# A recurrent two-layer kernel: how the first groups and the weight maxima are prepared

## Chip, cores and metric

One core of one Trainium2 chip. The metric is the device time of one execution in microseconds (us), the median of several runs; lower is better.

## What is computed

```python
xn = layernorm(x)                                   # x: 32 x 256 x 128, f32
s = L0_attn(xn)       # mix with previous row, k, v, r products, exp, decayed sums over time, Wo
g = silu(L0_ffn(xn))  # three products with weights of +1/-1 (bools k0, k1, k2), relu between
x = x + s * g
xn = layernorm(x)
s = L1_attn(xn)       # W_in, conv, silu, W_x, softplus step, scan over time, W_out
g = silu(L1_ffn(xn))  # shared and 4 of 16 routed experts, gelu
x = x + s * g
```

Layer 1's weights are scaled by powers of two and split into two halves of 16 bits. The power comes from a bound on a tensor's magnitude (`amax`, seven tensors: I_IN, I_UP, I_RW, I_WX, I_DT, I_CW, I_CB).

## The kernel before

The 8192 rows of x are 16 groups of 512, all kept in SBUF. Each engine has its own list of instructions, written by hand, tied by semaphores. `bodies` runs `layer0(n)` for 18 values of n: three written out, a loop for n = 3 to 14, three more. In a body n every engine does its part for group f = n (normalised rows, products, scans), for m = n - 1 (hidden layers 2 and 3 of the ffn, division by the sums) and t = n - 2 (result turned back and added). `between` puts extra steps behind a body: on VectorE `magnitudes` behind body 0 and `scales` behind body 2, on GpSimd `constants` behind body 1. `paired` then runs layer 1.

Names: `xn` normalised rows; `b_T` the PSUM bank they are turned into; `prev` and `xh`, ScalarE's copies from it; `xm` the mix (VectorE, L726), the operand of the k, v, r products; `xl` the low half of the turned rows. `hidden0` and `hidden1` are the ffn's products. `high` (ScalarE) and `low` (VectorE, L717) split their results. `Pk`, `Pv` are the scans (L759, L766), `gp` and `sg` the body's end on VectorE (L777, L781). `w0` is made of `k0_u` and the signs of `scal`; `w1`, `w2` by GpSimd.

The loads stand on three queues: SP (x, `wsq` = Wk, Wv, Wr, Wo, then k0, then layer 1's), ScalarE (small vectors), GpSimd (k1, k2). `wq_loaded` covers the four square weights and k0; `wa_loaded` all six small loads.

## Time and profile before

| | |
|---|---|
| median of 3 runs | 714.25 us (711.76 to 715.2) |
| the profiled execution | 714.81 us |
| its span | 713.0 us |
| TensorE, VectorE, ScalarE, GpSimd busy | 643.3, 636.2, 504.4, 281.5 us |
| mean granted clock | 0.97 of full |

The span runs from the first to the last instruction. Busy time can overlap between engines. An idle time stands in brackets before the row that ended it, with the one that released it.

### The profile page before, as it was taken

The numbers are of one execution on the slowest core, as the hardware profiler recorded it, in microseconds if no ns is written. First come the engines' busy times: TensorE is split into PE (matmuls) and PEld (weight loads), VectorE is DVE, ScalarE is ACT, GpSimd is POOL, SyncE is SP. The second block draws the span as 40 slices with busy tenths as digits, with TensorE's granted clock in tenths as the row PEclk, the third lists the DMA queues.
The fourth block names the chain that finished last, engine by engine and source line by source line (L and its number), as shares of the span: only waits on it lengthen the run. The fifth ranks groups of instructions, "written<-read, shape, count | busy, mean of one in ns | idle before, by whom it ended". The sixth has DMA issues, their size and how long they took to land. (4 is left out here: it accounts for less than half of the span.)

```text
span 713.0 us, 10841 instructions
## 1 busy us (share of the span) xinstructions
PE 643.3 (90%) x2711; PEld 306.4 (43%) x2711; DVE 636.2 (89%) x1467; ACT 504.4 (71%) x800; POOL 281.5 (39%) x278
## 2 busy tenths in 40 slices
PE   2796899999999997679999999999999999999985
PEld 1342344444444443324444444444444444444432
DVE  5896999999999998658999999999999999999876
ACT  2463566666666664279788878888797888788874
POOL 6456576677777664013221231223032213312220
PEclk9898999999999999569999999999999999999999
DMA  5431000000000000000000000000000000000000
GB/s 143 115 86 44 0 0 0 0 0 0 0 0 0 0 1 0 1 0 1 0 16 15 1 15 15 15 1 15 15 15 0 15 15 0 15 15 15 0 16 29
DMA packets 10739, 11.29 MB, mean 16 GB/s; under 512 B 4800, under 2 KB 6288, under 8 KB 10720
## 3 DMA queue, kind: packets, MB, share of 16 engines
q1 hardware_dynamic: 9744, 10.73, 5.1%
q0 software_dynamic: 112, 0.33, 0.2%
q8 instruction: 8, 0.13, 0.1%
q10 hardware_dynamic: 864, 0.00, 0.1%
q14 instruction: 11, 0.09, 0.0%
HBM read 6.87 MB, written 4.19 MB: 16 GB/s over the span
## 5 line engine op out<-in xcount | busy, mean ns | idle before, releaser
L1058 PE MATMUL bank<-arena,w 128*128 128x512 f16 x640 | 153.9, 389 | 19.8 <-DVE arena L717 14.1
L1058 PE MATMUL bank<-arena,dnT 128*128 128x512 f32 x288 | 138.6, 592 | 0.0
L613 ACT ACTIVATE arena<-bank,xinv 128x512 f32<-128x512 f32 x144 | 94.9, 687 | 39.0 <-PE bank L1058 38.8
L443 POOL TENSOR_TENSOR arena<-arena 128x512 f32<-128x512 f32 x48 | 59.7, 1274 | 137.8 <-ACT arena L550 137.8
L1058 PEld LDWEIGHTS bank<-arena,w 128*128 128x128 f16 x640 | 63.4, 100 | 98.8 <-issue 24.3
L476 ACT ACTIVATE arena<-bank 128x512 f16<-128x512 f32 x96 | 53.9, 606 | 35.1 <-PE bank L1058 35.1
L433 POOL TENSOR_TENSOR arena<-arena 128x512 f32<-128x512 f32 x16 | 17.1, 1067 | 150.1 <-DVE arena L917 150.1
L1058 PE MATMUL bank<-arena,wsqT 128*128 128x512 f32 x128 | 65.9, 619 | 6.0 <-DVE arena L726 6.0
L1058 PEld LDWEIGHTS bank<-arena,dnT 128*128 128x128 f32 x288 | 53.7, 191 | 35.9 <-issue 21.4
L926 DVE SCALAR_TENSOR_TENSOR arena<-bank,cws,arena 128x506 f32<-128x506 f32 (+1 forms) x96 | 67.1, 740 | 1.1
L717 DVE SCALAR_TENSOR_TENSOR arena<-bank,arena 128x512 f16<-128x512 f32 x96 | 60.2, 670 | 1.7 <-ACT arena L476 0.5
L938 DVE TENSOR_TENSOR arena<-arena 128x512 f32<-128x512 f32 x80 | 52.4, 689 | 0.0
L396 POOL TENSOR_TENSOR arena<-arena 128x512 f16<-128x512 f32 x32 | 36.9, 1155 | 29.7 <-ACT arena L476 22.9
L473 ACT ACTIVATE arena<-bank 128x512 f32<-128x512 f32 x32 | 19.1, 597 | 33.0 <-PE bank L1058 33.0
L400 POOL TENSOR_TENSOR arena<-arena 128x512 f32<-128x512 f32 x16 | 20.3, 1270 | 51.1 <-DVE arena L753 51.1
L979 DVE TENSOR_TENSOR_SCAN arena<-arena 128x256 f32<-128x256 f32 x64 | 38.9, 671 | 0.0
L1058 PE MATMUL bank<-arena,wcH 128*128 128x512 f16 x128 | 38.1, 379 | 0.0
L1058 PE MATMUL bank<-xh,upH 128*128 128x512 f16 x72 | 28.8, 401 | 8.3 <-ACT arena L613 4.8
L1058 PEld LDWEIGHTS bank<-arena,wsqT 128*128 128x128 f32 x128 | 25.4, 200 | 22.9 <-issue 9.7
L588 ACT ACTIVATE arena<-arena 128x512 f32<-128x512 f32 x32 | 20.2, 631 | 20.3 <-DVE arena L926 20.3
L1058 PE MATMUL bank<-arena,w_out 128*128 128x512 f32 x64 | 30.2, 594 | 3.1 <-DVE arena L986 3.1
L1058 PE MATMUL bank<-xh_,upH 128*128 128x512 f16 x72 | 27.4, 380 | 5.0 <-ACT arena L613 5.0
(208 smaller groups left out, 1519.5 us busy)
## 6 DMA issues: line engine op xcount, KB each, us to landing
x_all<-in_L_attn_x SPq DMA_DIRECT2D x16, 256.0 KB, 2.7
out<-x_all SPq DMA_DIRECT2D x16, 256.0 KB, 2.0
up_n<-in_L_ffn_routed_up SPq DMA_DIRECT2D x1, 512.0 KB, 3.9
dn_n<-in_L_ffn_routed_down SPq DMA_DIRECT2D x1, 512.0 KB, 5.4
wx<-in_L_attn_W_x SPq DMA_DIRECT2D x1, 288.0 KB, 3.0
k_u<-in_L_ffn_k POOLq DMA_DIRECT2D x1, 256.0 KB, 5.1
w_in<-in_L_attn_W_in SPq DMA_DIRECT2D x1, 256.0 KB, 2.7
k_u<-in_L_ffn_k SPq DMA_DIRECT2D x1, 128.0 KB, 5.6
```

The lines of the kernel that those rows point to most:

```text
L396: g.tensor_tensor(hl[:, 1, j, :], relu[:, j, :], hh[:, 1, j, :], ALU.subtract).then_inc(sem["a_low"], 1)
L400: g.tensor_tensor(ya[:, :], ysr[:, :], rec[:, :], ALU.mult).then_inc(sem["a_y"], 1)
L443: g.tensor_tensor(prod[:, c, :], act[:, c + 1, :], gate[:, :], ALU.mult).then_inc(sem["b_actp"], 1)
L473: a.activation(relu[:, j, :], src, ACT.Relu).then_inc(sem["a_relu"], 1)
L476: a.activation(hh[:, layer, j, :], src, ACT.Relu).then_inc(sem[("a_hi0", "a_hi1")[layer]], 1)
L588: a.activation(xc[:, par, k, :], u[:, k, :], ACT.Silu).then_inc(sem["b_xc"], 1)
L613: a.activation(act[:, c, :], q_U[(c + 1) % 2][:, :], ACT.Gelu, scale=xinv[:, I_UP:I_UP + 1]).then_inc(sem["b_act"], 1)
L717: v.scalar_tensor_tensor(hl[:, layer, j, :], b_Z[layer][j][:, :], 0.0, hh[:, layer, j, :], ALU.max, ALU.subtract).then_inc(sem[("a_lo0", " ...
L926: v.scalar_tensor_tensor(uk, seqs(q_U[k][:, :])[:, :, 0:T - back], cws[:, k, t:t + 1], uk, ALU.mult, ALU.add)\
L938: v.tensor_tensor(prod[:, c, :], act[:, c + 1, :], gate[:, :], ALU.mult).then_inc(sem["b_actg"], 1)
L979: last = v.tensor_tensor_scan(H[:, k, w], delta[:, k, w], bx[:, k, w], 0.0, ALU.mult, ALU.add)
L1058: return nc.tensor.matmul(ps, lhsT, rhs, start=start, stop=stop)
```

## The change

- Loads: `k0` is issued between Wv and Wr, with a semaphore of its own; Wr and Wo have one too. On ScalarE's queue the mix comes first, then the three scalars, then decay and first; each part has its semaphore.
- Group 0: GpSimd computes only rstd; VectorE normalises with four instructions.
- The square weights are turned in two halves, and ScalarE copies them out (VectorE did all four).
- In body 0, `w0` comes behind `xm` and `xl`; `high` and `low` of hidden layer 1 and the decays come ahead of the scans. ScalarE makes its channel factors behind `xh`.
- `up_n`, `rw_n` and `wdt` get as bound the sum of magnitudes in a partition (ScalarE, in body 1) instead of the maximum.
- GpSimd's `partition_all_reduce` goes. TensorE turns `amax` in body 1, VectorE takes the largest in each of seven rows and puts it on a diagonal, TensorE spreads it by a product with ones, VectorE copies it out. `scales` stands behind body 1 instead of body 2.

VectorE at the opening, before (`c` is c3, `w` is w0, the last row is xm):

```order
L700 TENSOR_SCALAR w0c<-sg_ 128x1
L701 TENSOR_TENSOR w0d<-k_u 128x512
L702 TENSOR_TENSOR sab<-scal,sg_ 128x2
L703 TENSOR_SCALAR w<-w0d,w0c 128x512
L704 TENSOR_TENSOR c<-sab 128x1
L706 COPY wsqT<-bank 128x512
L709 SCALAR_TENSOR_TENSOR c<-c,scal 128x1
L710 TENSOR_SCALAR dec<-ones,tch 128x128
L711 TENSOR_SCALAR dec<-ones,tch 128x128
L712 TENSOR_SCALAR c<-c 128x1
L726 SCALAR_TENSOR_TENSOR arena<-bank,chan,prev 128x512
```

and now:

```order
L734 TENSOR_SCALAR xn<-x_all,mv,rstd 128x128 x4
L740 TENSOR_SCALAR w1c<-sg_ 128x1
L741 TENSOR_SCALAR w1c<-sg_ 128x1
L742 TENSOR_TENSOR sab<-scal,sg_ 128x2
L743 TENSOR_SCALAR w0c<-sg_ 128x1
L746 TENSOR_TENSOR w0d<-k_u 128x512
L778 SCALAR_TENSOR_TENSOR arena<-bank,chan,prev 128x512
L781 SCALAR_TENSOR_TENSOR xl<-bank,xh 128x512
L752 TENSOR_SCALAR w<-w0d,w0c 128x512
L753 TENSOR_TENSOR c<-sab 128x1
```

Ahead of xm the copy of wsqT, w0, c3 and the decays are gone, and the normalising rows have come.

GpSimd from body 1 to body 2, before:

```order
L409 TENSOR_TENSOR arena<-arena,Pv 128x512
L412 TENSOR_TENSOR arena<-arena 128x512
L424 ISA
L424 ISA amax<-amax 128x7
L396 ISA
L396 TENSOR_TENSOR arena<-arena 128x512 x2
L400 TENSOR_TENSOR arena<-arena 128x512
```

and now:

```order
L422 TENSOR_TENSOR arena<-arena,Pv 128x512
L425 TENSOR_TENSOR arena<-arena 128x512
L409 TENSOR_TENSOR arena<-arena 128x512 x2
L413 TENSOR_TENSOR arena<-arena 128x512
L366 TENSOR_TENSOR ve<-mv,epsc 128x4
```

The reduction and the two other `ISA` rows around it are gone; the rest keeps its order.

The diff, cut to its core:

```diff
         loads_q = [(wsq[:, i, :], A["L0_attn_" + n]) for i, n in enumerate(("Wk", "Wv", "Wr", "Wo"))]
-        loads_q.append((k0_u[:, :, :], A["L0_ffn_k0"].rearrange("(k p) f -> p k f", p=P)))
+        loads_r = loads_q[2:]
+        loads_q = loads_q[:2]
+        load_k0 = (k0_u[:, :, :], A["L0_ffn_k0"].rearrange("(k p) f -> p k f", p=P))
+        load_mix = (chan[:, 2:3], A["L0_attn_time_mix"].rearrange("a b c -> c (a b)"))
         loads_a = [
-            (chan[:, 2:3], A["L0_attn_time_mix"].rearrange("a b c -> c (a b)")),
             (chan[:, 0:1], A["L0_attn_time_decay"]),
             (chan[:, 1:2], A["L0_attn_time_first"]),
         ]
-        loads_a += [(scal[:, i:i + 1], A["L0_ffn_" + n].partition_broadcast(P)) for i, n in enumerate(("s0", "s1", "s2"))]
+        loads_s = [(scal[:, i:i + 1], A["L0_ffn_" + n].partition_broadcast(P)) for i, n in enumerate(("s0", "s1", "s2"))]
...
+            sp.dma_start(*load_k0).then_inc(sem["k0_loaded"], 16)
+            for dst, src in loads_r:
+                sp.dma_start(dst, src).then_inc(sem["wr_loaded"], 16)
...
-                    pool.wait_ge(sem[ph + "centred"], n + 1)
+                    pool.wait_ge(sem[ph + "centred"], n)
...
-            normalise(0, "a_")
+            spread_of_rows(0, "a_")
...
-            def constants():
-
-                pool.wait_ge(sem["absmax_ready"], NSC)
-                g.partition_all_reduce(amax[:, :], amax[:, :], P, bass.bass_isa.ReduceOp.max).then_inc(sem["absmax_all"], 1)
-
-            bodies(pool, layer0, {1: constants, G - 1: lambda: spread_of_rows(0)})
+            bodies(pool, layer0, {G - 1: lambda: spread_of_rows(0, "b_")})
...
+            actv.dma_start(*load_mix).then_inc(sem["mix_loaded"], 16)
+            for dst, src in loads_s:
+                actv.dma_start(dst, src).then_inc(sem["scal_loaded"], 16)
             for dst, src in loads_a:
                 actv.dma_start(dst, src).then_inc(sem["wa_loaded"], 16)
-            actv.wait_ge(sem["wa_loaded"], WA_ALL)
-
+
+            def square_out(half):
+
+                actv.wait_ge(sem["square_turned"], half + 1)
+                a.activation(wsqT[:, 2 * half:2 * half + 2, :].rearrange("p a b -> p (a b)"),
+                             (b_S, b_F)[half][:, 0:2 * P], ACT.Copy).then_inc(sem["square_ready"], 1)
+
+            square_out(0)
+            actv.wait_ge(sem["scal_loaded"], WS_ALL)
             a.activation(sg_[:, :], scal[:, 0:2], ACT.Sign).then_inc(sem["signs_ready"], 1)
-            a.activation(tch[:, 0:1], chan[:, 0:1], ACT.Exp).then_inc(sem["chan_ready"], 1)
-            actv.wait_ge(sem["chan_ready"], 1)
-            a.activation(tch[:, 1:2], tch[:, 0:1], ACT.Exp, scale=-1.0).then_inc(sem["chan_ready"], 1)
-            a.activation(tch[:, 2:3], chan[:, 1:2], ACT.Exp).then_inc(sem["chan_ready"], 1)
             actv.wait_ge(sem["mix_ready"], 1)
 
+            def channel_factors():
+
+                actv.wait_ge(sem["wa_loaded"], WA_ALL)
+                a.activation(tch[:, 0:1], chan[:, 0:1], ACT.Exp).then_inc(sem["chan_ready"], 1)
+                actv.wait_ge(sem["chan_ready"], 1)
+                a.activation(tch[:, 1:2], tch[:, 0:1], ACT.Exp, scale=-1.0).then_inc(sem["chan_ready"], 1)
+                a.activation(tch[:, 2:3], chan[:, 1:2], ACT.Exp).then_inc(sem["chan_ready"], 1)
+                square_out(1)
...
+            def bounds():
+
+                flat = "p a b -> p (a b)"
+                actv.wait_ge(sem["wb_loaded"], WB_ALL)
+                actv.wait_ge(sem["const_ready"], 9)
+                for i, w, at in ((I_UP, up_n[:, :, :].rearrange(flat), 0), (I_RW, rw_n[:, :], UC * P),
+                                 (I_DT, wdt[:, :], (UC + 1) * P)):
+                    a.activation(absw[0:w.shape[0], at:at + w.shape[1]], w, ACT.Abs,
+                                 accum_out=amax[0:w.shape[0], i:i + 1]).then_inc(sem["absmax_ready"], 1)
...
+                    if isinstance(f, int) and f == 0:
+                        channel_factors()
...
+                if isinstance(f, int) and f == 1:
+                    bounds()
                 if has(m):
                     high(1, m, 2)
+                if isinstance(f, int) and f == 0:
+                    for j in range(FC):
+                        high(0, 0, j)
...
-            dve.wait_ge(sem["wa_loaded"], WA_ALL)
+            dve.wait_ge(sem["mix_loaded"], 16)
             v.tensor_scalar(tch[:, 3:4], chan[:, 2:3], -1.0, 1.0, ALU.mult, ALU.add).then_inc(sem["mix_ready"], 1)
 
+            def normalised(n, ph):
+
+                dve.wait_ge(sem[ph + "rstd"], n + 1)
+                after(dve, sem[ph + "xnT"], n)
+                for j in range(J):
+                    last = v.tensor_scalar(xn[:, j, :], x_all[:, bass.ds(n * N + j * P, P)], mv[:, j, 0:1],
+                                           rstd[:, j:j + 1], ALU.subtract, ALU.mult)
+                last.then_inc(sem[ph + "xn"], 1)
+
+            normalised(0, "a_")
             dve.wait_ge(sem["signs_ready"], 1)
             v.tensor_scalar(w1c[:, 0:1], sg_[:, 1:2], 2.0 * W1S, None, ALU.mult)
             v.tensor_scalar(w1c[:, 1:2], sg_[:, 1:2], -W1S, None, ALU.mult).then_inc(sem["w1_ready"], 1)
-            dve.wait_ge(sem["wq_loaded"], WQ_ALL)
-
-            links(v.tensor_scalar(w0c[:, :], sg_[:, 0:1], 2.0 * W0S, None, ALU.mult),
-                  v.tensor_tensor(w0d[:, :], k0_u[:, 0, :], k0_u[:, 1, :], ALU.subtract),
-                  v.tensor_tensor(sab[:, :], scal[:, 0:2], sg_[:, :], ALU.mult))
-            links(v.tensor_scalar(w0[:, :], w0d[:, :], w0c[:, 0:1], None, ALU.mult),
-                  v.tensor_tensor(c3[:, 0:1], sab[:, 0:1], sab[:, 1:2], ALU.mult))
-            dve.wait_ge(sem["square_turned"], 1)
-            v.tensor_copy(wsqT[:, :, :].rearrange("p a b -> p (a b)"), b_S[:, :]).then_inc(sem["square_ready"], 1)
-            dve.wait_ge(sem["const_ready"], 7)
-            dve.wait_ge(sem["chan_ready"], 3)
-            links(v.scalar_tensor_tensor(c3[:, 1:2], c3[:, 0:1], FS, scal[:, 2:3], ALU.mult, ALU.mult),
-                  v.tensor_scalar(dec[:, 0:P], ones[:, :], tch[:, 1:2], None, ALU.mult),
-                  v.tensor_scalar(dec[:, P:T], ones[:, 0:T - P], tch[:, 1:2], None, ALU.mult))
-            v.tensor_scalar(c3[:, 2:3], c3[:, 1:2], 0.5, None, ALU.mult).then_inc(sem["const_done"], 1)
+            v.tensor_tensor(sab[:, :], scal[:, 0:2], sg_[:, :], ALU.mult)
+            v.tensor_scalar(w0c[:, :], sg_[:, 0:1], 2.0 * W0S, None, ALU.mult).then_inc(sem["signs_used"], 1)
+            dve.wait_ge(sem["const_ready"], 5)
+            dve.wait_ge(sem["k0_loaded"], 16)
+            v.tensor_tensor(w0d[:, :], k0_u[:, 0, :], k0_u[:, 1, :], ALU.subtract).then_inc(sem["k0_joined"], 1)
+
+            def signed_weights():
+
+                dve.wait_ge(sem["signs_used"], 1)
+                dve.wait_ge(sem["k0_joined"], 1)
+                links(v.tensor_scalar(w0[:, :], w0d[:, :], w0c[:, 0:1], None, ALU.mult),
+                      v.tensor_tensor(c3[:, 0:1], sab[:, 0:1], sab[:, 1:2], ALU.mult))
+                v.scalar_tensor_tensor(c3[:, 1:2], c3[:, 0:1], FS, scal[:, 2:3], ALU.mult,
+                                       ALU.mult).then_inc(sem["const_done"], 1)
+
+            def decays():
+
+                dve.wait_ge(sem["const_ready"], 7)
+                dve.wait_ge(sem["chan_ready"], 3)
+                dve.wait_ge(sem["const_done"], 1)
+                v.tensor_scalar(c3[:, 2:3], c3[:, 1:2], 0.5, None, ALU.mult)
+                v.tensor_scalar(dec[:, 0:P], ones[:, :], tch[:, 1:2], None, ALU.mult)
+                v.tensor_scalar(dec[:, P:T], ones[:, 0:T - P], tch[:, 1:2], None, ALU.mult).then_inc(sem["const_done"], 1)
...
+                    if isinstance(f, int) and f == 0:
+                        v.scalar_tensor_tensor(xl[:, :], b_T[:, :], XS, xh[:, :], ALU.mult,
+                                               ALU.subtract).then_inc(sem["a_xl"], 1)
+                        signed_weights()
...
+                if isinstance(f, int) and f == 0:
+                    for j in range(FC):
+                        low(0, 0, j)
+                    decays()
+                    dve.wait_ge(sem["const_done"], 2)
...
+                if isinstance(f, int) and f == 1:
+                    largest()
...
-                for i, w in ((I_IN, w_in[:, :]), (I_UP, up_n[:, :, :].rearrange(flat)), (I_RW, rw_n[:, :]),
-                             (I_WX, wx[:, :, :].rearrange(flat)), (I_DT, wdt[:, :]),
+                for i, w in ((I_IN, w_in[:, :]), (I_WX, wx[:, :, :].rearrange(flat)),
                              (I_CW, cw[:, :, :].rearrange(flat)), (I_CB, cb[:, :])):
                     v.tensor_reduce(amax[0:w.shape[0], i:i + 1], w, AX.X, ALU.max,
                                     apply_absolute_value=True).then_inc(sem["absmax_ready"], 1)
 
+            def largest():
+
+                dve.wait_ge(sem["absmax_turned"], 1)
+                link(v.tensor_reduce(amx[0:NSC, :], b_S[0:NSC, 0:P], AX.X, ALU.max))
+                v.tensor_scalar(adiag[0:NSC, :], ident[0:NSC, 0:NSC], amx[0:NSC, 0:1], None,
+                                ALU.mult).then_inc(sem["absmax_diag"], 1)
...
+                dve.wait_ge(sem["absmax_spread"], 1)
+                v.tensor_copy(amax[:, :], b_RX[:, 0:NSC]).then_inc(sem["absmax_all"], 1)
                 dve.wait_ge(sem["absmax_all"], 1)
...
-            bodies(dve, layer0, {0: magnitudes, 2: scales, G - 1: matrices, G: turned_matrices})
+            bodies(dve, layer0, {0: magnitudes, 1: scales, G - 1: matrices, G: turned_matrices})
...
-            for i in range(4):
-                last = nc.tensor.transpose(b_S[:, i * P:(i + 1) * P], wsq[:, i, :], ident[:, :])
-            last.then_inc(sem["square_turned"], 1)
+
+            def square_turned(half):
+
+                for i in range(2):
+                    last = nc.tensor.transpose((b_S, b_F)[half][:, i * P:(i + 1) * P], wsq[:, 2 * half + i, :], ident[:, :])
+                last.then_inc(sem["square_turned"], 1)
+
+            square_turned(0)
...
+                if isinstance(f, int) and f == 0:
+                    pe.wait_ge(sem["wr_loaded"], WR_ALL)
+                    square_turned(1)
...
+                    if isinstance(t, int) and t == 0:
+                        pe.wait_ge(sem["absmax_all"], 1)
...
+                if isinstance(f, int) and f == 1:
+                    pe.wait_ge(sem["absmax_ready"], NSC)
+                    pe.wait_ge(sem["square_ready"], 1)
+                    nc.tensor.transpose(b_S[0:NSC, 0:P], amax[:, :], ident[:, :]).then_inc(sem["absmax_turned"], 1)
...
+                    if isinstance(f, int) and f == 0:
+                        pe.wait_ge(sem["square_ready"], 2)
...
                     last.then_inc(sem["a_f"], 1)
                 if has(m):
                     pe.wait_ge(sem["a_y"], m + 1)
+                    if isinstance(m, int) and m == 0:
+                        pe.wait_ge(sem["absmax_diag"], 1)
                     after(pe, sem["a_sg"], m)
                     mm(b_S[:, :], wsqT[:, 3, :], ya[:, :]).then_inc(sem["a_s"], 1)
+                if isinstance(f, int) and f == 1:
+                    pe.wait_ge(sem["a_thr"], 2)
+                    mm(b_RX[:, 0:NSC], ones[0:NSC, :], adiag[0:NSC, :]).then_inc(sem["absmax_spread"], 1)
```

## Rows read from the trace of the kernel before

**Rows 1.** The page: busy time of the engines, and TensorE's granted clock in 40 slices.
```profile
PE 643.3 (90%) x2711; PEld 306.4 (43%) x2711; DVE 636.2 (89%) x1467; ACT 504.4 (71%) x800; POOL 281.5 (39%) x278
...
PEclk9898999999999999569999999999999999999999
```

**Rows 2.** Timeline of the loop: start us, us, engine, line, operation, [idle before].
```profile
103.41 0.75 DVE L726 SCALAR_TENSOR_TENSOR arena<-bank,chan,prev 128x512 f32<-128x512 f32 x1 [0.22 <-ACT xh L486]
...
117.03 0.66 PE L1069 MATMUL bank<-ident,xn 128*128 128x128 f32 x4 [0.60 <-POOL xn L368]
...
118.93 0.75 DVE L726 SCALAR_TENSOR_TENSOR arena<-bank,chan,prev 128x512 f32<-128x512 f32 x1 [0.21 <-ACT xh L486]
```

**Rows 3.** Timeline of VectorE, opening.
```profile
8.86 0.15 DVE L693 TENSOR_SCALAR tch<-chan 128x1 f32<-128x1 f32 x1 [3.74 <-DMA scal<-in_L_ffn_s]
...
10.08 2.09 DVE L703 TENSOR_SCALAR w<-w0d,w0c 128x512 f16<-128x512 f32 x1
...
13.93 0.74 DVE L726 SCALAR_TENSOR_TENSOR arena<-bank,chan,prev 128x512 f32<-128x512 f32 x1
```

**Rows 4.** Timeline of VectorE, end of body 0.
```profile
23.16 2.45 DVE L717 SCALAR_TENSOR_TENSOR arena<-bank,arena 128x512 f16<-128x512 f32 x4
...
26.13 1.34 DVE L791 TENSOR_REDUCE amax<-up_n 128x1 f32<-128x1152 f32 x1
...
28.70 0.73 DVE L726 SCALAR_TENSOR_TENSOR arena<-bank,chan,prev 128x512 f32<-128x512 f32 x1
```

**Rows 5.** Timeline of all engines, body 2.
```profile
45.15 0.75 DVE L726 SCALAR_TENSOR_TENSOR arena<-bank,chan,prev 128x512 f32<-128x512 f32 x1 [0.21 <-ACT xh L486]
...
61.23 3.77 PE L1058 MATMUL bank<-arena,w 128*128 128x512 f16 x8 [5.65 <-POOL arena L396]
...
65.76 0.69 DVE L777 SCALAR_TENSOR_TENSOR gp<-thf,bank 128x512 f32<-128x512 f32 x1 [6.69 <-ACT thf L520]
...
67.15 0.94 DVE L807 SCALAR_TENSOR_TENSOR bnd<-amax 128x1 f32<-128x1 f32 x1
...
72.72 0.75 DVE L726 SCALAR_TENSOR_TENSOR arena<-bank,chan,prev 128x512 f32<-128x512 f32 x1
...
73.53 1.98 PE L1058 MATMUL bank<-arena,wsqT 128*128 128x512 f32 x4 [1.96 <-DVE arena L726]
```

**Rows 6.** Timeline of GpSimd, TensorE and ScalarE, opening.
```profile
6.59 1.03 POOL L363 TENSOR_TENSOR xn<-x_all,mv 128x512 f32<-128x512 f32 x1
7.77 1.04 POOL L368 TENSOR_TENSOR xn<-xn,rstd 128x512 f32<-128x512 f32 x1
...
9.63 1.06 PE L1069 MATMUL bank<-ident,xn 128*128 128x128 f32 x4
...
11.38 0.59 ACT L486 ACTIVATE xh<-bank 128x512 f16<-128x512 f32 x1
...
14.73 4.49 PE L1058 MATMUL bank<-arena,wsqT 128*128 128x512 f32 x6 [4.04 <-DVE arena L726]
```

**Rows 7.** Timeline of GpSimd around its reduction over partitions.
```profile
52.69 0.40 POOL L424 PARTITION_ALL_REDUCE amax<-amax  x1 [5.86 <-issue]
59.95 1.14 POOL L396 TENSOR_TENSOR arena<-arena 128x512 f16<-128x512 f32 x1 [6.86 <-issue]
```

**Rows 8.** Timeline of VectorE: four normalising instructions, beside GpSimd's and alone.
```profile
277.49 2.79 DVE L891 TENSOR_SCALAR xn<-x_all,mv,rstd 128x128 f32<-128x128 f32 x4 [1.41 <-POOL rstd L419]
...
330.42 1.11 DVE L891 TENSOR_SCALAR xn<-x_all,mv,rstd 128x128 f32<-128x128 f32 x4
```

**Rows 9.** Instructions of L759: duration ns min/median/max, first and last start us.
```profile
L759 DVE TENSOR_TENSOR_SCAN Pk<-dec,arena x32: 660/682/1461, 19.1 to 268.4; 128x256 f32<-128x256 f32 x32
```

**Rows 10.** Body 1: timeline of TensorE and ScalarE; windows, with the granted clock before DMA share.
```profile
25.76 6.55 PE L1058 MATMUL bank<-arena,w 128*128 128x512 f16 x16 [4.38 <-DVE arena L717]
...
35.79 0.60 ACT L476 ACTIVATE arena<-bank 128x512 f16<-128x512 f32 x1 [1.70 <-PE bank L1058]
...
25.00:26.00 1.00, 0.24 (x1) 0.14 (x2) 1.00 (x3) 0.00 (x0) 0.90 (x1) 0.50 0.00 0
```

More of the change, by code:

```diff
@@ L507, in layer0 @@
                     a.activation(thr[:, :], b_RX[:, :], ACT.Tanh, scale=0.5).then_inc(sem["a_thr"], 1)
-                    high(0, f, 0)
+                    if not (isinstance(f, int) and f == 0):
+                        high(0, f, 0)
                     actv.wait_ge(sem["a_thr"], f + 1)
@@ L511, in layer0 @@
                     a.activation(sr[:, :], thr[:, :], ACT.Copy, scale=0.5, bias=0.5).then_inc(sem["a_sr"], 1)
-                    high(0, f, 1)
-                    high(0, f, 2)
-                    high(0, f, 3)
+                    if not (isinstance(f, int) and f == 0):
+                        high(0, f, 1)
+                        high(0, f, 2)
+                        high(0, f, 3)
                 if has(m):
@@ L732, in layer0 @@
                         dve.wait_ge(sem["bn_done"], f + 2)
-                    after(dve, sem["a_z0"], FC * f)
-                    v.scalar_tensor_tensor(xl[:, :], b_T[:, :], XS, xh[:, :], ALU.mult, ALU.subtract).then_inc(sem["a_xl"], 1)
+                    if not (isinstance(f, int) and f == 0):
+                        dve.wait_ge(sem["a_z0"], FC * f)
+                        v.scalar_tensor_tensor(xl[:, :], b_T[:, :], XS, xh[:, :], ALU.mult,
+                                               ALU.subtract).then_inc(sem["a_xl"], 1)
                     if ahead:
@@ L768, in layer0 @@
                     last.then_inc(sem["a_scanV"], 1)
+                if has(f) and not (isinstance(f, int) and f == 0):
                     low(0, f, 0)
                     low(0, f, 1)
-                if has(f):
                     low(0, f, 2)
@@ L884, in turned_low @@
                 v.scalar_tensor_tensor((xl, xl_)[par][:, :], ps[:, :], XS, (xh, xh_)[par][:, :], ALU.mult, ALU.subtract).then_inc(sem["b_xl"], 1)
-            def normalised(n):
-                dve.wait_ge(sem["b_rstd"], n + 1)
-                after(dve, sem["b_xnT"], n)
-                for j in range(J):
-                    last = v.tensor_scalar(xn[:, j, :], x_all[:, bass.ds(n * N + j * P, P)], mv[:, j, 0:1],
-                                           rstd[:, j:j + 1], ALU.subtract, ALU.mult)
-                last.then_inc(sem["b_xn"], 1)
-            bodies(dve, layer0, {0: magnitudes, 2: scales, G - 1: matrices, G: turned_matrices})
+            bodies(dve, layer0, {0: magnitudes, 1: scales, G - 1: matrices, G: turned_matrices})
             def top_four(n):
@@ L1018, in layer1 @@
                 if ahead:
[L1019 removed]
+                    normalised(f + 1, "b_")
                 if has(m):
```

32 lines of the change are left out of this document (16 added, 16 removed).

## The prediction

> **What bounds the kernel now.** I read the busy shares and slices first [rows 1]. TensorE and VectorE are each busy for nine tenths of the span. The granted clock of TensorE is at or near full in all 40 slices but those at the change of layers, with lower digits in the first slices too. So I asked where the first 75 us differ from the loop of layer 0. In the loop, the addition that makes xm (L726) comes every 15.52 us [rows 2]. I use this instruction on VectorE as the mark of a body: it starts body 0 at 13.93, body 1 at 28.70, body 2 at 45.15 and body 3 at 72.72 [rows 3 to 5]. The bodies before the loop thus take 14.77, 16.45 and 27.57 us. Two losses stand out. The first mark comes only at 13.93, though xn was ready at 7.77 + 1.04 = 8.81 and xh at 11.38 + 0.59 = 11.97 [rows 6]: VectorE was busy with weights. And body 2 is 12 us longer than a loop body. There GpSimd's reduction over partitions stands with 5.86 us of idle time before it and 6.86 after it, both put down to "issue" and not to another engine [rows 7]. Behind it TensorE waits 5.65, and VectorE 6.69 [rows 5]. After these, VectorE's chain of scales runs from 67.15 to the mark at 72.72, some 5.5 us [rows 5].
>
> Nothing after body 3 is changed but the order of source lines. A body there is held by the engines, not by loads, so I take what is gained up to body 3 to be gained at the end. The change is therefore summed at the marks.
>
> **1. The first mark.** Rstd is there at 6.59, where GpSimd's own subtraction starts [rows 6]. GpSimd then took 2.2 us for two steps. VectorE's four instructions take 1.11 us when left alone and 2.79 at worst, at a place where GpSimd worked beside them [rows 8]. GpSimd now clears buffers at that time, so I take 1.6, with 1.1 and 2.8 as ends: xn at 8.2. TensorE no longer turns four square matrices just before (two are turned earlier, since it waits for Wk and Wv only); turning xn takes 1.06 and ended at 10.69 [rows 6], so 9.4. ScalarE's two passes end 11.97 - 10.69 = 1.3 later, at 10.7. VectorE has by then only small instructions and w0d behind it, and w0, with its 2.09 us [rows 3], stands after xm and xl. Mark 0 comes at 10.9 instead of 13.93: **-3.0** (-1.8 to -3.6). This needs the signs, whose three loads are now issued second to fourth in ScalarE's queue; before they landed by 8.86 at the latest [rows 3], and even that would be no later than 8.9.
>
> **2. Body 0.** Xm ends at 11.6, and three f32 products take 4.3 to the first hidden one, as before (14.73 to 19.05, by the 4.49 of its six records) [rows 6]: 16.0. The first hidden product and ScalarE's half bring low() to 17.1; four of them take 2.45 [rows 4] and now stand ahead of the scans: 19.5. The decay tables, 0.6, make 20.1. Four scans take 0.66 to 1.46 each [rows 9], 2.6 to 4.2 in all; I take 3.3: 23.4. The seven maxima took 28.70 - (23.16 + 2.45) = 3.1. Three of them, with 1152 + 128 + 256 = 1536 elements a partition, go to ScalarE; the largest took 1.34 [rows 4], so the three some 1.8, and about 1.4 is left. Mark 1: 24.9, a body of 14.0 instead of 14.77: **-0.8** (-1.7 to +0.2). Hidden products of body 1 wait for low(), 19.5 instead of 25.61, so that TensorE is idle for about 1 us where it was for 4.4 [rows 10].
>
> **3. Body 1 without scales.** Sixteen hidden products took 6.55 us there at the clock of 0.50 [rows 10]; with the shorter gap they should keep full clock. Then the body is a loop body, 15.5. Added on VectorE are largest() (two tiny instructions of some 0.15 [rows 3] and two waits, 0.5), on TensorE a turn of seven columns and a 7-column product (under 0.5 together). ScalarE's three sums of magnitudes have 1536 elements. By the 0.60 us of 512 elements they cost 1.8; they stand where ScalarE sat idle for 1.70 [rows 10], so 0 to 0.5 of it shows. Body 1: 16.0 instead of 16.45: **-0.45** (-0.9 to +0.5).
>
> **4. Scales come before mark 2.** The copy from PSUM adds 0.3. The chain took 5.5, partly since small instructions were held while GpSimd worked: one of a single element took 0.94 [rows 5], another such 0.15 [rows 3]. With its four long ones at 0.15, it would be some 2.1. After sg of body 1 GpSimd still has two or three instructions to run, so I take 4.3: **+4.6** (+2.4 to +5.8).
>
> **5. Body 2.** 27.57 less the chain of 5.5 and the idle 6.7 leaves 15.3, which agrees with a loop body: **-12.3** (-12.0 to -12.5). GpSimd's reduction is gone from the program, not moved, as the order of GpSimd's instructions shows. This is the term that carries the rest, so its cause matters. The row shows one idle stretch ahead of the reduction and one behind it, 12.7 us with nothing to wait for, and the next instruction, at 59.95, is what TensorE waited for. The Trainium skill, "GPSIMD Engine Reference", section "Instruction dispatch", prices the first call of a freshly loaded kernel at about 6 us, with no instruction in the profile. It names one such load, so by it alone GpSimd would be free at about 53, no engine would have waited, and the saving would be near 6 us less; the trace shows the second stretch as well and decides.
>
> Sum: -3.0 - 0.8 - 0.45 + 4.6 - 12.3 = **-11.95**. The profiled execution took 714.81 us (span 713.0), so 702.9. That run stands 0.56 above the median of 714.25, so the forecast for the median is **702.3 us**. Loads have slack: those of stage two are issued when s1W is cleared, now some 2 us earlier, since GpSimd no longer normalises first, and the maxima ask for them about 2 us earlier. They are hidden in both; if one landed later, body 0 would stretch by its lateness.
>
> **Rivals.**
> *A: the clock falls in the gap of the scales.* After sg TensorE has at most sixteen hidden products and a turn left. Sixteen at full clock take half of 6.55, 3.3; part of the first eight is done by then, so 2.9, while VectorE needs 0.3 + 4.3 + 0.75 to the next xm: idle 2.5 us. At mark 3 TensorE waited 1.96, and its next products ran at 1.98 for four records [rows 5]; a wait of 4.4 was followed by 0.50 [rows 10]. The gap lies between. If the clock falls, a stretch like the 6.55 of sixteen products is half lost, 3.3 at most; with some slack I take 2.5: 702.3 + 2.5 = 704.8. The Trainium skill, "TensorE: Matmul & The Clock Gate", section "HAM oscillation — how this bites in real kernels", says that waits of a kernel can bring the clock down again after each burst; the two rows above agree.
> *B: the start gains little.* If the signs land late or xn is held by the clears, terms 1 and 2 shrink to 1: 705.
> *C: the reduction's stall was not all code loading.* If something of GpSimd's after it is still late, say half of it, the gain is 5 to 6: 708.5.
> *D, slower: the loop runs in a worse phase.* In the loop TensorE waits 0.60 for xn and VectorE 0.21 for xh in each body [rows 2]. The engines hand over in a circle (xn, turned rows, xm, low), and a different entry could settle at another period, say with xn late by one GpSimd instruction (1.04 us [rows 6]). Over 12 loop bodies a period above 16.5 would take all of the 12 us; at 16.6 the time is 715.3. Against it: body 1, whose clock was down, and body 2, whose GpSimd stood still, both led into a loop of one period, so the circle sets it and not its entry.
> *E: no effect,* the saved time is waited for elsewhere, in the change of layers. Its code there waits for no load that lands so late.
>
> **How the numbers follow.** The forecast with its own range, 699.5 to 704: 0.55. A 0.20, B 0.10, C 0.08, D 0.03, E 0.04. The bounds of the terms, if all fall the same way, sum to -16.3 and -7.3, which is 698.0 and 707.0 for the median. I take these as the range: it holds the forecast, A and B, and leaves out C, D and E (0.15). Half a per cent, 3.6 us, is about what a measurement can tell from no change. Faster by more (below 710.7): 0.93; within: 0.04; slower: 0.03.
>
> **What would show it.** The marks should stand near 10.9, 24.9, 45.5 and 60.8. GpSimd's row should have no idle of "issue" over 5 us. VectorE's gap of 6.69 before gp should be gone, hidden products of body 1 should take 3.6 and not 6.55 for 16, and loop marks should stay 15.52 apart. I am wrong if mark 3 is later than 65, or if the loop's period moves by over 0.1 us.

## The result, and the profile after

The changed kernel takes **701.83 us** (median of 4 runs, 700.39 to 703.48) where the kernel before takes 714.25. The ratio of the two, taken over their runs, is 0.9839, with a 95% interval of 0.9803 to 0.9875 (the two medians alone divide to 0.983). The forecast was 702.3 with a range of 698 to 707. The profiled execution took 703.48 us; its span is 701.7, where that of before was 713.0. One run of `reduction_back` (812.34 us, mean granted clock 0.829) was in a slower state of the chip and is left out of its numbers below.

The page, busy time and granted clock, for comparison with [rows 1]:

```profile
PE 641.6 (91%) x2714; PEld 305.8 (44%) x2714; DVE 631.5 (90%) x1470; ACT 507.1 (72%) x808; POOL 279.7 (40%) x275
...
PEclk9999999999999997679999999999999999999999
```

No engine does much less than before: VectorE 4.7 us less, TensorE 1.7. Most of the 11.3 us is idle time that went: 9.6 us of TensorE's, 6.6 of VectorE's. The marks (start of the xm instruction on VectorE, now L778) say where. Timeline of VectorE, the marks of bodies 0 to 4, against [rows 3 to 5]:

```profile
10.75 0.75 DVE L778 SCALAR_TENSOR_TENSOR arena<-bank,chan,prev 128x512 f32<-128x512 f32 x1 [0.68 <-ACT xh L511]
...
25.83 0.73 DVE L778 SCALAR_TENSOR_TENSOR arena<-bank,chan,prev 128x512 f32<-128x512 f32 x1
...
45.92 0.74 DVE L778 SCALAR_TENSOR_TENSOR arena<-bank,chan,prev 128x512 f32<-128x512 f32 x1
...
61.01 0.75 DVE L778 SCALAR_TENSOR_TENSOR arena<-bank,chan,prev 128x512 f32<-128x512 f32 x1 [0.22 <-ACT xh L511]
...
76.53 0.75 DVE L778 SCALAR_TENSOR_TENSOR arena<-bank,chan,prev 128x512 f32<-128x512 f32 x1 [0.22 <-ACT xh L511]
```

| stretch | before | forecast | after |
|---|---|---|---|
| start to mark 0 | 13.93 | 10.9 | 10.75 |
| body 0 | 14.77 | 14.0 | 15.08 |
| body 1 (the scales stand here now) | 16.45 | 20.6 | 20.09 |
| body 2 (they stood here before) | 27.57 | 15.3 | 15.09 |
| body 3 | 15.16 | as before | 15.52 |
| sum, mark 4 | 87.88 | | 76.53 (-11.35) |

The loop's bodies stay 15.52 us apart, and the whole run is 714.81 - 703.48 = 11.33 shorter: between these two profiles nothing is gained or lost behind mark 4 (626.93 us from there to the end before, 626.95 after). So the time came from body 2 (-12.5) and the opening (-3.2), and body 1, which now holds the scales, took 3.6 of it back.

GpSimd's timeline shows the two idle stretches of [rows 7] gone. Its last instruction of body 1 and the first behind it:

```profile
41.31 1.27 POOL L425 TENSOR_TENSOR arena<-arena 128x512 f32<-128x512 f32 x1
44.83 1.15 POOL L409 TENSOR_TENSOR arena<-arena 128x512 f16<-128x512 f32 x1 [2.24 <-ACT arena L491]
```

It waits 2.24 us, and for ScalarE's data instead of for "issue". The chain of scales on VectorE, its first and its last instruction, the one long one:

```profile
42.98 0.16 DVE L880 SCALAR_TENSOR_TENSOR bnd<-amax 128x1 f32<-128x1 f32 x1
...
44.88 1.12 DVE L897 SCALAR_TENSOR_TENSOR fac<-fac,inv 128x1 f32<-128x1 f32 x1
```

From 42.98 to the mark at 45.92 it takes 2.94, where it took 5.57 before (67.15 to 72.72). Only one of its 16 instructions is held, and that one lies exactly beside GpSimd's at 44.83: they end at 46.00 and 45.98. The other 15 take 0.12 to 0.23 each.

One thing in the profile was not forecast. Timeline of TensorE in bodies 0 and 1, and windows of 1 us (the granted clock stands before the DMA share):

```profile
11.55 5.49 PE L1122 MATMUL bank<-arena,wsqT 128*128 128x512 f32 x6 [1.15 <-DVE arena L778]
...
20.82 3.61 PE L1122 MATMUL bank<-arena,w 128*128 128x512 f16 x16 [1.56 <-DVE arena L769]
26.62 3.18 PE L1122 MATMUL bank<-arena,wsqT 128*128 128x512 f32 x4 [2.18 <-DVE arena L778]
29.60 4.15 PE L1122 MATMUL bank<-arena,w 128*128 128x512 f16 x16
```

```profile
27.00:28.00 1.00, 1.00 (x3) 0.33 (x2) 0.48 (x3) 0.00 (x0) 1.00 (x2) 0.63 0.57 215
28.00:29.00 1.00, 1.00 (x3) 0.37 (x2) 1.00 (x6) 0.87 (x2) 1.00 (x2) 0.50 0.03 8
29.00:30.00 1.00, 1.00 (x2) 0.15 (x1) 1.00 (x1) 1.00 (x4) 0.44 (x1) 0.50 0.44 154
```

The sixteen hidden products of body 1 run at full clock, as hoped (3.61 instead of 6.55). But VectorE still has scans and maxima to do, TensorE waits 2.18 for xm, and the clock then falls to its lower level, 1.2 GHz (0.50 in the windows), under the k product. And the three f32 products of body 0 took 5.49 where the same six records had 4.49 before [rows 6].

### The profile page after: what moved, and what is told of

The parts are those of the page before. It is cut to its first block and busy times, and to the rows that moved or that the text cites. A ratio compares the mean times of both kernels' runs of the same rounds, so it can differ in the third digit from the quotient of the medians.

```text
span 701.7 us, 10854 instructions
## 1 busy us (share of the span) xinstructions
PE 641.6 (91%) x2714; PEld 305.8 (44%) x2714; DVE 631.5 (90%) x1470; ACT 507.1 (72%) x808; POOL 279.7 (40%) x275
## 5 line engine op out<-in xcount | busy, mean ns | idle before, releaser
L1122 PE MATMUL bank<-arena,w 128*128 128x512 f16 x640 | 149.7, 382 | 12.9 <-DVE arena L769 12.9
L1122 PE MATMUL bank<-arena,wsqT 128*128 128x512 f32 x128 | 67.6, 634 | 4.4 <-DVE arena L778 4.4
L368 POOL TENSOR_TENSOR rstd<-ve,neghalf 128x4 f32<-128x4 f32 x32 | 36.4, 1136 | 2.5
```

Source lines behind the costliest of these rows:

```text
L368: g.tensor_tensor(rstd[:, :], ve[:, :], neghalf[:, :], ALU.pow).then_inc(sem[ph + "rstd"], 1)
L1122: return nc.tensor.matmul(ps, lhsT, rhs, start=start, stop=stop)
```

## The experiments

The kernel before, measured beside them, had medians of 714.37 (13 runs) for the first four, 713.31 (11 runs) for the next four, and 710.2 (one run) for the last four. So times of different groups are compared by their ratios to it, and only with care by themselves.

### The reduction put back

`reduction_back` is the changed kernel with the reduction of before:

```diff
-            bodies(pool, layer0, {G - 1: lambda: spread_of_rows(0, "b_")})
+            bodies(pool, layer0, {1: constants, G - 1: lambda: spread_of_rows(0, "b_")})
...
-            bodies(dve, layer0, {0: magnitudes, 1: scales, G - 1: matrices, G: turned_matrices})
+            bodies(dve, layer0, {0: magnitudes, 2: scales, G - 1: matrices, G: turned_matrices})
```

`constants` is that of before; TensorE's turn and spreading, largest() and the copy are left out.

> The changed kernel with GpSimd's reduction over partitions back behind body 1 and the scales behind body 2; all else stays changed, the sums of magnitudes on ScalarE too. Theory (the stall is made by the reduction alone, its 5.86 and 6.86 us of issue around it): GpSimd shows both stretches again, mark 3 comes some 12 to 13 us after that of the changed kernel less the moved chain, so near 69 to 70, and the time is 710 to 711. Rival (the new opening had already made room, so the reduction would now be hidden): under 705. Rival (the opening carries the gain): 702.

Measured: 707.87 us (three runs, 706.95 to 708.12), ratio 0.9905 (0.987 to 0.9939), and marks at 10.59, 25.48, 42.37 and 68.83. Mark 3 is 7.8 us behind that of the changed kernel. Timeline of GpSimd, and mark 3 on VectorE:

```profile
48.32 0.40 POOL L430 PARTITION_ALL_REDUCE amax<-amax  x1 [6.16 <-issue]
56.04 2.26 POOL L409 TENSOR_TENSOR arena<-arena 128x512 f16<-128x512 f32 x2 [7.32 <-issue]
```

```profile
68.83 0.75 DVE L783 SCALAR_TENSOR_TENSOR arena<-bank,chan,prev 128x512 f32<-128x512 f32 x1
```

Both stretches are back. Mark 3 came within 0.2 us of its forecast; the time came lower than forecast by more than 2 us. The trace says where: layer 1's code is the same, but the stretch from its first product to the first of its second group took 18.37 us in this execution and 21.27 in the profile of the changed kernel. A mark's gain or loss does not reach the end whole in every execution (more on this in the last section).

### The reduction exchanged alone

`reduction_only` is the kernel before, with nothing but the reduction taken over from the change (turn, largest(), spreading, copy) and the scales behind body 1. Opening, loads and maxima are those of before.

> The kernel before with only the reduction exchanged for the turn, the largest, the diagonal and the spread, and the scales behind body 1; opening, maxima and body 0 as before. Theory: marks 0 and 1 stay at 13.93 and 28.70, mark 3 comes at about 64, the time is 714.3 less 8 to 9, so 705 to 706. Rival (reduction and opening only pay together): 710 or more.

Measured: 704.8 us (702.48 to 707.07), ratio 0.9857 (0.9822 to 0.9893). Marks 0 and 1 stayed, at 13.79 and 28.45. Timeline of VectorE, marks 2 and 3:

```profile
49.31 0.74 DVE L723 SCALAR_TENSOR_TENSOR arena<-bank,chan,prev 128x512 f32<-128x512 f32 x1
...
64.41 0.75 DVE L723 SCALAR_TENSOR_TENSOR arena<-bank,chan,prev 128x512 f32<-128x512 f32 x1 [0.22 <-ACT xh L483]
```

Mark 3 is 72.72 - 64.41 = 8.3 us earlier. With the 3.9 that `reduction_back` has at its mark 3 (72.72 - 68.83), the two halves give 12.2; the whole change gave 72.72 - 61.01 = 11.7. So the parts hardly touch each other, and the exchange of the reduction, with the move of the scales that it allows, is worth two thirds and more of the change at the marks.

### The reduction done twice

`reduction_twice` is the kernel before with the reduction's line written twice, one behind the other; VectorE's scales wait for both:

```diff
                 g.partition_all_reduce(amax[:, :], amax[:, :], P, bass.bass_isa.ReduceOp.max).then_inc(sem["absmax_all"], 1)
+                pool.wait_ge(sem["absmax_all"], 1)
+                g.partition_all_reduce(amax[:, :], amax[:, :], P, bass.bass_isa.ReduceOp.max).then_inc(sem["absmax_all"], 1)
```

> The kernel before with the reduction written twice in a row (the second leaves the maxima as they are). If the 5.86 and 6.86 us are paid at the change between GpSimd's own code and the reduction's, once in and once out, the second costs about its 0.4 us: 714.5 to 715.5. If each reduction pays them, a second costs 12 us more: 726 to 727. If the stretch behind is the reduction's own unseen work, it comes again and the stretch ahead does not: some 721.

Measured: 714.06 us (10 runs), ratio 1.0009 (0.9991 to 1.0028). Timeline of GpSimd:

```profile
51.28 0.40 POOL L424 PARTITION_ALL_REDUCE amax<-amax  x1 [5.77 <-issue]
51.78 0.38 POOL L426 PARTITION_ALL_REDUCE amax<-amax  x1
59.45 2.26 POOL L396 TENSOR_TENSOR arena<-arena 128x512 f16<-128x512 f32 x2 [7.29 <-issue]
```

The second reduction takes 0.38 us and has no stretch of its own. So the price is not that of a reduction. It is paid on the way into this kind of instruction (5.8 to 6.2 us in these profiles) and once more on the way back to ordinary ones (6.9 to 7.3). The unnamed `ISA` rows in the order of GpSimd's instructions before stand at these two places, one ahead of the reduction and one ahead of L396. What GpSimd does in the stretches no profile shows, and no run shows whether a later reduction, with ordinary instructions between, pays the first stretch again. Here a reduction of seven columns held GpSimd for 13 us.

### All maxima on VectorE

`maxima_vector` is the changed kernel with the three sums taken from ScalarE; VectorE takes all seven maxima again behind body 0.

> The changed kernel with all seven maxima on VectorE, true maxima as before. Theory: mark 1 comes 1.8 us later (27.6 instead of 25.83), TensorE waits longer before the k product of body 1, and the time rises by 1 to 2 us to 703 to 704. Rival (mark 1 is set by TensorE's slow products, VectorE had room): no change, 701.8.

Measured: 705.59 us (700.08 to 708.59), ratio 0.9875 (0.9813 to 0.9938), too wide to part it from the changed kernel by time. The trace is clearer. From the first maximum to mark 1 VectorE needs 26.59 - 23.45 = 3.14, in the changed kernel 25.83 - 24.46 = 1.37: 1.77 us less. Mark 1 came only 0.76 later, though, and not the 1.8 of the theory, since the first three products took 4.59 in this execution and not 5.49. This was the first sign that a part of body 0 differs from one execution to the next. TensorE's wait before the k product grew from 2.18 to 3.95, as the theory had it, and mark 3 came at 62.71, 1.70 later.

### The scales one body later

`scales_late` leaves the copy from PSUM behind body 1, and puts the chain of scales behind body 2.

> The changed kernel with the chain of scales behind body 2 again, where it stood before; the copy of the spread maxima stays behind body 1. Theory of the forecast (the chain's length is a matter of what GpSimd runs beside it): in the changed kernel it took 2.94 us (42.98 to 45.92), at the old place it takes 3 to 5.5, mark 3 comes 0 to 2.5 us later, and the time is 702 to 704. Rival (the place does not matter, each body has the same slack): same chain, same time within 0.5.

Measured: 704.66 us (703.1 to 707.53), ratio 0.9875 (0.9837 to 0.9914). Timeline of VectorE, the chain's long instructions and mark 3:

```profile
57.24 0.64 DVE L883 SCALAR_TENSOR_TENSOR bnd<-amax 128x1 f32<-128x1 f32 x1
...
58.02 1.22 DVE L885 TENSOR_TENSOR bnd<-bnd,amax 128x1 f32<-128x1 f32 x1
...
59.68 0.97 DVE L889 TENSOR_SCALAR inv<-pow 128x7 f32<-128x7 f32 x1
...
61.70 0.75 DVE L778 SCALAR_TENSOR_TENSOR arena<-bank,chan,prev 128x512 f32<-128x512 f32 x1
```

GpSimd beside it:

```profile
56.69 1.18 POOL L422 TENSOR_TENSOR arena<-arena,Pv 128x512 f32<-128x512 f32 x1
57.95 1.27 POOL L425 TENSOR_TENSOR arena<-arena 128x512 f32<-128x512 f32 x1
59.48 1.15 POOL L409 TENSOR_TENSOR arena<-arena 128x512 f16<-128x512 f32 x1 [0.26 <-ACT arena L491]
```

The same chain takes 61.70 - 57.24 = 4.46 us here and 2.94 in the changed kernel, with the same instructions. In its place behind body 2, GpSimd works at 56.69 to 60.6 with one gap of 0.26; behind body 1 it sits idle from 42.58 to 44.83. And the three long instructions end at 57.88, 59.24 and 60.65, where GpSimd's end at 57.87, 59.22 and 60.63. The four long ones of the kernel before end in the same way, 0.01 to 0.02 us behind one of GpSimd's each (68.09 behind 68.08, 72.00 behind 71.98). So an instruction of VectorE is held until GpSimd's is through, and what the chain costs is set by what GpSimd does beside it. Which of the small instructions are held and which pass beside a running one of GpSimd, these rows do not explain.

### Keeping TensorE's clock up

Three kernels add unused products, whose results nothing reads. `warm_opening` has ten products of the identity by itself before TensorE's first turn; `warm_both` has also eight f16 products ahead of the k product of body 1; `warm_all` has also 32 where TensorE is idle at the change of layers, and 14 ahead of the first expert:

```diff
+            for _ in range(10):
+                mm(b_Z0[:, 0:P], ident[:, :], ident[:, :])
...
+                if isinstance(f, int) and f == 1:
+                    for _ in range(8):
+                        mm(b_F[:, :], w1[:, 0, 0:P], hh[:, 0, 0, :])
...
+                if isinstance(f, int) and f == G:
+                    for _ in range(32):
+                        mm(b_T[:, :], w1[:, 0, 0:P], hh[:, 0, 0, :])
...
+                if isinstance(f, int) and f == 0:
+                    for _ in range(14):
+                        mm(q_F[:, :], upH[:, 0:P], XH[:, :])
```

> The changed kernel with ten products of ident with itself (f32, 128 columns, into a bank that is free) on TensorE between ident and the first turned weights; their result is not used. Theory (body 0 was 1 us longer than forecast since the three f32 products ran at half rate, 0.86 us from record to record, after an opening with no products): the products take 2.6 to 4.5 us instead of 5.3, mark 1 comes 0.8 to 2.5 us earlier, mark 3 as much. Rival (the engine slows again before 11.55, or low() and the scans wait for ScalarE): marks unchanged.

> As warm_opening, and eight unused f16 products ahead of the k product of body 1, where the changed kernel shows a granted clock of 0.50 from 28 to 30. Theory: that clock stays 1.00, the k and v products take 1.9 instead of 3.2 us, low() of body 1 does not wait 0.73 us for ScalarE, and mark 2 comes 0.5 to 1 us earlier than in warm_opening. Rival (VectorE sets body 1 alone): mark 2 as in warm_opening.

> As warm_both, and 32 unused products in the gap of the change of layers (TensorE idle 7.86 us before 278.48 in the changed kernel), 14 before the first expert of layer 1. Theory (runs of one kernel differ by 3 us with the mean granted clock, 0.977 against 0.984, and the marks of layer 0 do not move, so the change of layers is where they differ): the clock stays up through it, the time falls by 2 to 4 us against warm_both, to 695 to 698, and its runs spread by less than 2 us. Rival (VectorE bounds the change of layers): under 1 us.

| kernel | median us | runs | ratio to before (95%) |
|---|---|---|---|
| `warm_opening` | 701.4 | 699.91 to 703.07 | 0.9841 (0.9811 to 0.987) |
| `warm_both` | 698.94 | 697.74 to 700.25 | 0.98 (0.9772 to 0.9828) |
| `warm_all` | 698.29 | 698.03 to 698.75 | 0.9795 (0.9768 to 0.9821) |

In the first profile of `warm_opening` the clock stayed full in body 1 and mark 3 came at 58.76, 2.25 us before that of the changed kernel. Yet its ratio, 0.9841, was no better than the changed kernel's 0.9839. `warm_both` had mark 2 at 43.59 and `warm_opening` at 43.66: no gain there, but both profiles had full clock in body 1, so the pair does not test its theory. `warm_all` fills the gap at the change of layers. Timeline of TensorE there, the changed kernel first and `warm_all` second:

```profile
278.48 1.89 PE L1122 MATMUL bank<-arena,w 128*128 128x512 f16 x4 [7.86 <-DVE arena L769]
280.16 1.92 PE L1122 MATMUL bank<-arena,wsqT 128*128 128x512 f32 x2
```

```profile
275.55 1.20 PE L1122 MATMUL bank<-arena,w 128*128 128x512 f16 x4 [0.96 <-DVE arena L769]
276.59 1.02 PE L1122 MATMUL bank<-arena,wsqT 128*128 128x512 f32 x2
```

The idle 7.86 is filled, and the two products behind it take 1.02 instead of 1.92. The clock does not stay up through the whole change of layers, though: it reads 0.50 from 282 to 288. The six runs of `warm_all` lie within 0.7 us, where those of every other kernel but `reduction_back` (1.2) spread over 2.5 us and more. Its median is the lowest, but only 0.65 under that of `warm_both`, as the rival had it, and the intervals of these two overlap almost wholly. Measured at the same time, each of its six runs lies under the lowest of `warm_opening` (699.91), so unused products do pay once they stand in the later gaps too. That it beats the changed kernel itself is likely and not shown: they were not measured together, and the intervals 0.9768 to 0.9821 and 0.9803 to 0.9875 overlap a little.

### The same kernels profiled again

`warm_opening` had an earlier mark 3 and yet no better median, so both kernels were profiled again. `after_again` and `after_third` are the changed kernel, `warm_again` and `warm_third` are `warm_opening`, all with nothing edited.

> The changed kernel unchanged, profiled again. Four kernels with the same opening show the three f32 products of body 0 with 5.49, 5.35, 4.77 and 4.59 us for the same six records. Theory V (the step to full rate comes at a time that varies from one execution to the next): the row again lies between 4.5 and 5.5, another value than 5.49, and mark 1 moves by the difference, 24.9 to 25.8. Theory F (it belongs to the code): 5.4 to 5.5 and mark 1 at 25.8 again. Body 1: a granted clock of 0.50 for 2 us or more between 26 and 31, by both.

> As after_again, a third profile of the changed kernel. Theory V: the products' row between 4.5 and 5.5; theory F: 5.4 to 5.5. The clock's fall in body 1 is there again if it belongs to the code.

> The kernel of warm_opening (ten unused products ahead of the first turns), profiled again. If the unused products are what keeps body 1 at full clock: no 1 us window under 1.00 between 24 and 32, first three products 4.5 to 4.6, mark 3 at 58.5 to 59.0, 2 us before the changed kernel's. If it was luck: a fall in one of the two profiles, and products of up to 5.5.

> As warm_again, a third profile of it: full clock in body 1 and mark 3 at 58.5 to 59.0 by the one theory, a fall and mark 3 at 60 to 61 by the other.

| profile | us | three f32 products of body 0 | clock of 0.50 between marks 1 and 2 | marks 1, 2, 3 | body 1 |
|---|---|---|---|---|---|
| after | 703.48 | 5.49 | 27 to 31 | 25.83, 45.92, 61.01 | 20.09 |
| `after_again` | 700.71 | 4.69 | 39 to 43 | 24.86, 43.33, 58.43 | 18.47 |
| `after_third` | 701.91 | 5.30 | 26 to 31 | 25.52, 45.61, 60.70 | 20.09 |
| `warm_opening` | 699.98 | 4.54 | none | 24.27, 43.66, 58.76 | 19.39 |
| `warm_again` | 703.71 | 4.54 | 25 to 29 | 24.39, 44.48, 59.58 | 20.09 |
| `warm_third` | 699.61 | 2.84 | 24 to 28 | 23.22, 43.31, 58.41 | 20.09 |
| `warm_both` | 700.25 | 4.49 | none | 24.20, 43.59, 58.69 | 19.39 |
| `warm_all` | 698.11 | 4.54 | 39 to 43 | 24.51, 42.97, 58.08 | 18.46 |

The rows of body 0 in the changed kernel, 5.49, 4.69 and 5.30, bear out theory V: the same code takes different times.

Timeline of TensorE, the f32 products of bodies 0 and 1, in `after_again`:

```profile
11.44 4.69 PE L1122 MATMUL bank<-arena,wsqT 128*128 128x512 f32 x6 [1.03 <-DVE arena L778]
...
25.65 1.98 PE L1122 MATMUL bank<-arena,wsqT 128*128 128x512 f32 x4 [2.18 <-DVE arena L778]
```

in `warm_again`:

```profile
11.12 4.54 PE L1122 MATMUL bank<-arena,wsqT 128*128 128x512 f32 x6 [1.42 <-DVE arena L778]
...
25.18 3.68 PE L1122 MATMUL bank<-arena,wsqT 128*128 128x512 f32 x4 [2.19 <-DVE arena L778]
```

and in `warm_third`:

```profile
10.94 2.84 PE L1122 MATMUL bank<-arena,wsqT 128*128 128x512 f32 x6 [1.90 <-DVE arena L778]
...
24.01 3.45 PE L1122 MATMUL bank<-arena,wsqT 128*128 128x512 f32 x4 [2.18 <-DVE arena L778]
```

The reader should compare the brackets: TensorE waits 2.18 or 2.19 for the k product of body 1 in every one of them, and what follows runs at full clock in one execution (1.98) and mostly at half in the next (3.45, 3.68). The same code and the same wait give either. The early fall is thus no property of the changed kernel; it came in two of its three profiles, and in two of the three of `warm_opening`. That products in the opening keep body 1 at full clock, as the first profile of `warm_opening` suggested, is refuted with it. What they do change in each of its three profiles is the first turns (two square turns 0.38 instead of 0.69) and mark 0, 10.14 to 10.31 instead of 10.64 to 10.75; a gain of that size is under what the medians can show. The products of `warm_both` stand in the gap itself, which leaves 0.46 of it, and in both profiles with them (`warm_both`, `warm_all`) the k product runs at full clock; two profiles are too few to say that it always does.

The third profile of the changed kernel without an early fall, `after_again`, is not at full clock throughout. There the clock falls later in body 1, behind waits of 1.07 and 0.89 us; the same fall stands in `warm_all`, while the same two waits led to none in `warm_opening`. TensorE and GpSimd in `after_again`, and window 40 to 41:

```profile
39.49 3.37 PE L1122 MATMUL bank<-arena,w 128*128 128x512 f16 x8 [0.89 <-DVE arena L769]
...
44.23 1.16 POOL L409 TENSOR_TENSOR arena<-arena 128x512 f16<-128x512 f32 x1 [2.72 <-ACT arena L491]
```

```profile
40.00:41.00 1.00, 1.00 (x4) 0.35 (x3) 0.93 (x4) 0.00 (x0) 0.92 (x2) 0.50 0.68 156
```

Eight hidden products take 3.37 there and 1.90 in the profile of after. Yet body 1 is shortest in these two executions, 18.5 us, and not in the two at full clock, 19.39. The cause is the chain of scales. In `warm_opening`, at full clock, GpSimd gets its data in time to start in the middle of the chain, and VectorE is held; VectorE and GpSimd there:

```profile
42.29 1.05 DVE L893 TENSOR_TENSOR fac<-inv,bnd 128x1 f32<-128x1 f32 x1
```

```profile
42.17 1.15 POOL L409 TENSOR_TENSOR arena<-arena 128x512 f16<-128x512 f32 x1 [1.25 <-ACT arena L491]
```

With slow products GpSimd's data come late, it starts at 44.23 when the chain has ended, and the chain takes 2.41 instead of 3.33. So three lengths of body 1 occur in the eight profiles: 20.09 with the early fall, 19.39 with none, 18.5 with the late one.

## Why the prediction was right, step by step

- **Term 1, the first mark (-3.0):** measured -3.2. VectorE's four normalising instructions took 1.62 us (forecast 1.6). Xn was ready at 8.1 and its turn began at 8.38, ScalarE's xh came at 10.13 + 0.59, and mark 0 at 10.75. Two of the inputs were off without harm: Wv now landed 6.2 us after its issue and not 3.0 (4.6 and 4.8 in the other two profiles), so the two square matrices that "are turned earlier" began only at 7.90; and VectorE waited 0.68 for xh. No run separates the parts of the opening (order of loads, normalising on VectorE, w0 behind xm); what each gives is read from the trace alone.
- **Term 2, body 0 (-0.8):** +0.3, the one term with the wrong sign in the profiled execution. Its failed step is "three f32 products take 4.3 to the first hidden one, as before". They took 16.84 - 11.55 = 5.3. In `after_again` they took 4.69 for the row, and body 0 had 24.86 - 10.64 = 14.2, against the forecast 14.0. So the mechanism holds, and the size of this step has an uncertainty of some 1 us that one profile of before could not show. The rest of the term came in: four scans 3.3 (3.3), from 21.16 to 24.46, the remaining maxima 1.37 (1.4).
- **Term 3, body 1 without scales (16.0):** 42.79 - 25.83 = 17.0 to the copy. In `warm_opening`, at full clock, 40.14 - 24.27 = 15.9, as forecast. The difference of 1.1 is the price of the early fall. At mark 2 it is 0.7 (20.09 against 19.39), since the chain is then held less. ScalarE's three sums were all hidden, as taken: they ran from 28.62 to 30.56, and ScalarE still waited 1.50 behind them. Largest() took 0.9 instead of 0.5, one of its two instructions (0.65) being held beside GpSimd.
- **Term 4, the scales (+4.6):** 0.2 for the copy and 2.94 for the chain, 3.1 in all (2.6 in `after_again`, 3.5 in `warm_opening`). This is the mis-sized term, by 1.5. "With its four long ones at 0.15" was the right reading of the row, but I then added back 2.2 of the 3.4 us that these had lost, for a GpSimd at work, while GpSimd sat idle for 1.85 of the chain's 2.94 us (until 44.83). `scales_late`, with GpSimd at work, had 4.46, near the 4.3 that I had put here.
- **Term 5, body 2 (-12.3):** -12.5. The wait of 6.69 and the chain went, and nothing took their place. A part that the term does not name is the clock: behind the wait of 5.65, which the reduction caused, eight hidden products took 3.77 [rows 5] and now take 1.90, 1.9 us on the way to VectorE's gp. The weighing of the two stretches came out right. The Trainium skill, "GPSIMD Engine Reference", section "Instruction dispatch", prices the first call of a freshly loaded kernel at about 6 us; the first stretch, 5.8 to 6.2 us here, agrees in size. The second one, of 6.9 to 7.3, is as real, and `reduction_twice` shows that a call directly behind the first pays neither.
- **Left out:** body 3 took 15.52 and not 15.16, +0.36. The old value was shorter than a loop body; I carried it over unchanged.

Terms 2, 3 and "left out" were 1.1, 1.0 and 0.4 too low, and term 4 1.5 too high; terms 1 and 5 gave 0.4 more. These cancel to 0.6, and that is why the sum of -11.95 stands so near to the -11.33 measured. A part of the nearness is luck. So is a part of the step from mark 4 to the end: the forecast took it as unchanged, and it was, to 0.02 us, in this pair of profiles, but over the 14 profiles of this case it runs from 624.1 to 628.9 us with the code behind mark 4 all but the same (only `warm_all` adds products there).

Of the rivals, **A** (the clock falls in the gap of the scales) did not happen where I put it: behind the scales TensorE waits 1.06 and the clock stays full. It fell in the same body all the same, in each of the three profiles of the changed kernel: twice at the wait of 2.18 ahead of the k product, which costs 0.7 us at mark 2 and not 2.5, and once just ahead of the scales, where it cost nothing and shortened the chain. **B** is refuted by terms 1 and 2, 2.9 us together and not 1. **C** is refuted by body 2, 15.09. **D** (another period of the loop): it is still 15.52. **E** is refuted for this pair of profiles by the end, where all of mark 4's gain is left; in `reduction_back` 2.8 us of a loss was made up behind mark 4.

## What to carry to other kernels

A tiny instruction can be dear through what surrounds it: read the idle time before and behind it, with its releaser, before its own duration. Here 0.40 us of work held an engine for 13, and a turn, two small VectorE instructions, a product with ones and a copy did the same in under 2 us of engine time. A small instruction is also dear by its neighbour: VectorE's were held to the end of GpSimd's, so a slower TensorE, which fed GpSimd later, made body 1 shorter. And before a difference of 1 or 2 us between two profiles is given a cause, profile the same kernel again: a mark that moves by 2.5 us between executions of one kernel can carry any story.

## What the runs showed of the hardware

- GpSimd's change of kind costs twice: 5.8 to 6.2 us into the reduction and 6.9 to 7.3 back out, as "issue"; a second reduction in a row takes 0.38.
- A small instruction of VectorE takes 0.12 to 0.23 us, or up to 1.22 when it is held beside a 128x512 instruction of GpSimd; the held ones of the chain, in three kernels, end 0.01 to 0.02 us behind GpSimd's.
- The granted clock as recorded is not complete in the first 18 us of a run. In the profile of after it reads 1.00 there, while the six f32 records take 5.49 us; the same records take 2.84 in `warm_third`. In `warm_opening`, with 4.54, it does read 0.50 from 12 to 14. Durations, not the clock's row, tell the rate there.
- The time of an execution often goes with its mean granted clock: `reduction_only` had 702.48 us at 0.987 and 707.07 at 0.977. It need not: `warm_both` had its longest run, 700.25 us, at 0.984 and its 698.97 at 0.977.
- The spread between executions of one kernel arises at few places. They are bodies 0 and 1, the change of layers with the first group of layer 1, and the end; the groups between keep their length to 0.05 us. In the three profiles of the changed kernel the first product of layer 1 starts at 289.82, 287.25 and 288.70, and 413.7, 413.5 and 413.2 us are left from there to the end. That these agree is chance: the first group takes 21.27, 19.63 and 19.48 us, and the last one, to the end of the span, 47.9, 49.3 and 49.3. In `warm_again`, with the same code there, 416.3 us are left.
- ScalarE's sum along a row shows as an extra row. Timeline of ScalarE, the first of the three sums:

```profile
28.62 1.16 ACT L500 ACTIVATE absw<-up_n 128x1152 f32<-128x1152 f32 x1
29.68 0.19 ACT L500 ACTIVATION_READ_ACCUMULATOR absw<-up_n 128x1 f32 x1
```

The reading of the sum takes 0.19, and the sum over 1152 elements 1.16, where VectorE's maximum of the same tensor took 1.34 [rows 4].
